# Quantised FFN, first half: groups in pairs, Gelu over two banks, rows normalised and put on the grid by GpSimd

## What is computed

```python
x = x + tanh(g_ffn[0]) * ffn(layernorm(x))
# ffn, with quantize_a16(v) = round(v * 32767 / max|v|) / (32767 / max|v|)
x_sim = quantize_a16(x)
hidden = gelu(x_sim @ W_in_sim + b_in)        # 128 -> 512
hidden_sim = quantize_a16(hidden)
out = hidden_sim @ W_out_sim + b_out          # 512 -> 128
```

## Time and profile before

| What | us |
|---|---|
| Median of 3 runs | 1489.21 (1488.17 to 1489.25) |
| Span of the profiled execution | 1487.2 |
| First half and its scale, steps at the start to the maximum (L1400 to L1427) | 616.2 to 677.1 |
| Second half (L1433 to L1444) | 678.7 to 738.5 |
| Busy over the span: TensorE, VectorE, ScalarE, GpSimd | 1444.1, 1064.9, 923.1, 640.4 |

### The profile page before, as it was taken

The page is one execution under the profiler, slowest core; times in us unless marked ns, Lnnn a source line. Parts: engine busy times, 40 slices in busy tenths (PEclk is TensorE's granted clock), DMA queues, the critical chain, the costliest instruction groups (busy, mean ns, idle before and its releaser), DMA issues. The chain is left out here.

```text
span 1487.2 us, 27490 instructions
## 1 busy us (share of the span) xinstructions
PE 1444.1 (97%) x9366; PEld 1209.9 (81%) x9384; DVE 1064.9 (72%) x2311; ACT 923.1 (62%) x1924; POOL 640.4 (43%) x755
## 2 busy tenths in 40 slices
PE   9999999999999999879999999999999999999997
PEld 8888888888888887639978888888888888778886
DVE  5677877666767678798566666666767676776887
ACT  4666666666666665496456666666666666556663
POOL 1333344343433334556023434343333333455885
PEclk9999999999999999999999999999999999999999
DMA  7655544444444442300055444444444444320011
GB/s 226 192 178 161 165 132 153 137 145 144 140 146 138 153 130 85 91 1 1 12 183 165 135 157 133 157 129 161 134 159 132 154 129 151 109 79 8 29 35 43
DMA packets 202786, 182.70 MB, mean 123 GB/s; under 512 B 12368, under 2 KB 201808, under 8 KB 202640
## 3 DMA queue, kind: packets, MB, share of 16 engines
q1 hardware_dynamic: 202080, 180.91, 38.7%
q10 hardware_dynamic: 576, 0.13, 0.1%
HBM read 95.74 MB, written 85.25 MB: 122 GB/s over the span
## 5 line engine op out<-in xcount | busy, mean ns | idle before, releaser
L1131 POOL TENSOR_TENSOR PN<-E,RC 128x512 f32<-128x512 f32 x378 | 331.2, 904 | 491.9 <-DVE RC L1089 491.9
L1038 DVE TENSOR_REDUCE MX<-pS 128x6 f32<-128x462 f32 (+1 forms) x384 | 222.6, 580 | 265.4 <-PE pS L657 265.4
L772 ACT ACTIVATE G<-pP 128x308 f32<-128x308 f32 (+1 forms) x488 | 208.9, 428 | 226.8 <-PE pP L525 226.5
L695 PE MATMUL pO<-work,PT 128*128 128x128 f32 (+1 forms) x2560 | 328.3, 276 | 4.1 <-ACT PT L856 4.1
L657 PE MATMUL pS<-G,XT 128*128 128x462 f32 (+1 forms) x768 | 321.0, 507 | 0.0
L695 PEld LDWEIGHTS pO<-work,PT 128*128 128x128 f32 (+1 forms) x2560 | 307.7, 192 | 8.4 <-issue 5.8
L847 ACT ACTIVATE E<-E 128x462 f32<-128x462 f32 (+1 forms) x384 | 209.6, 546 | 136.5 <-DVE E L1048 128.2
L523 PE MATMUL pP<-Chi,Ahi 128*128 128x308 f32 x496 | 235.2, 474 | 1.4 <-ACT G L772 1.2
L1048 DVE TENSOR_TENSOR E<-pS,MX 128x462 f32<-128x462 f32 (+1 forms) x384 | 223.6, 582 | 8.9
L856 ACT ACTIVATE PT<-pT 128x512 f32<-128x512 f32 (+1 forms) x384 | 200.2, 522 | 30.2 <-PE pT L680 28.7
L1086 DVE TENSOR_REDUCE SM<-E 128x16 f32<-128x1232 f32 (+1 forms) x144 | 184.8, 1290 | 44.7 <-ACT E L847 43.6
(11 more groups left out here) (241 smaller groups left out, 2032.7 us busy)
## 6 DMA issues: line engine op xcount, KB each, us to landing
values<-ST SPq DMA_DIRECT2D x256, 256.0 KB
work<-values SPq DMA_DIRECT2D x512, 128.0 KB
values<-ST SPq DMA_DIRECT2D x64, 208.0 KB
work<-values SPq DMA_DIRECT2D x128, 104.0 KB
C<-in_ctx SPq DMA_DIRECT2D x32, 154.0 KB
X<-in_x SPq DMA_DIRECT2D x16, 256.0 KB, 5.0
out<-s_O SPq DMA_DIRECT2D x16, 256.0 KB, 2.3
work<-in_L_xattn_Wq SPq DMA_DIRECT2D x2, 512.0 KB, 5.9
```

Of the source, the lines that this page charges most:

```text
L695: last = nc.tensor.matmul(pO[:, 0:CH], PT[0:rows, c, :], V[(t - 1) % VRING][0:rows, tile, CH * hh:CH * hh + CH], start=c == 0, stop=c == C ...
L772: return nc.scalar.activation(G[0:live, g % 2, :, head, :], bank[0:live, 0:KEYCOLS].rearrange("p (b k) -> p b k", k=KEYS), ACT.Copy)
L1038: nc.vector.tensor_reduce(MX[:, h0:h1], pS[u][:, 0:(h1 - h0) * KEYS].rearrange("p (h k) -> p h k", k=KEYS), X_AXIS, ALU.max).then_inc(max_ ...
L1131: nc.gpsimd.tensor_tensor(out, e, scale, ALU.mult).then_inc(prob_ready, 1)
```

## The change

The groups are taken in eight pairs. The sixteen up matmuls of a pair go chunk by chunk, four into two neighbouring banks `pU[c % 2]`, of which there are two sets instead of four single banks; a chunk waits for the Gelu two chunks back. One Gelu reads the 1024 columns of both banks: 32 in place of 64. Of `HI` and `LO` there are four each in place of two. TensorE turns the next pair's groups behind chunks 0 and 1, and ScalarE's `high` for them stands behind Gelus 0 and 1.

GpSimd writes each row block of 128 channels by one instruction with two values per partition (plus the negated mean, times the inverse deviation) straight into `XQ`, and then, in place over 512 columns, times the scale plus `ROUND`, which VectorE did before. The negated means are one more instruction at the start (`minus`). `XN` is gone. Groups 0 and 1 are normalised ahead of the scale.

VectorE's loop now is `low(g)`, `largest(g - 4)` for g from 2 to 15, then two more `largest`, then four reductions of 1024 columns (both groups of the last pair, a chunk each).

```diff
@@ -1211,29 +1211,31 @@
         small = sb("small", [128, 1])
         gbias = sb("gbias_f0", [128, CH])
         brow = sb("brow_f0", [128, CH])
-        amax = sb("amax", [128, GROUPS - 1 + FC])
+        PAIRS = GROUPS // 2
+        amax = sb("amax", [128, 2 * (PAIRS - 1) + FC])
+        minus = sb("minus", [128, BATCH])
 
         def half_of(i, first, n):
             return HALVES[:, i, 512 * first:512 * (first + n)]
 
-        XN = [half_of(0, i, 1).rearrange("p (b d) -> p b d", d=CH) for i in range(2)]
-        XQ = [half_of(0, 2 + i, 1).rearrange("p (b d) -> p b d", d=CH) for i in range(2)]
-        HI = [half_of(1, i, 1).bitcast(BF16)[:, 0:512] for i in range(2)]
-        LO = [half_of(1, i, 1).bitcast(BF16)[:, 512:1024] for i in range(2)]
+        XQ = [half_of(0, i, 1).rearrange("p (b d) -> p b d", d=CH) for i in range(2)]
+        parts = [half_of(0, 2, 1), half_of(0, 3, 1), half_of(1, 0, 1), half_of(1, 1, 1)]
+        HI = [h.bitcast(BF16)[:, 0:512] for h in parts]
+        LO = [h.bitcast(BF16)[:, 512:1024] for h in parts]
         raw_fc = half_of(1, 2, 1).rearrange("p (c d) -> p c d", d=CH)
         raw_proj = half_of(1, 3, 1)
         HQ = [HALVES[:, i, :].rearrange("p (c n) -> p c n", c=FC) for i in range(2)]
 
         pX = [s.enter_context(nc.psum_tensor(f"u_px{i}", [128, 512], F32)) for i in range(2)]
-        pU = [s.enter_context(nc.psum_tensor(f"u_pu{i}", [128, 512], F32)) for i in range(FC)]
+        pU = [s.enter_context(nc.psum_tensor(f"u_pu{i}", [128, 2, 512], F32)) for i in range(2)]
         pF = s.enter_context(nc.psum_tensor("pF", [128, 512], F32))
         pP = s.enter_context(nc.psum_tensor("pP", [128, 512], F32))
-        pD = pU[0:2]
+        pD = [pU[0][:, i, :] for i in range(2)]
 
...
@@ -1254,19 +1256,30 @@
         def _(pool):
             def normalise(g):
 
-                half, rows = g % 2, slice(g * GROUP, (g + 1) * GROUP)
                 if g >= 2:
-                    pool.wait_ge(xq_ready, g - 1)
-                nc.gpsimd.tensor_tensor(XN[half], p["X"][:, rows, :], p["mv"][:, rows, 0:1].to_broadcast([128, GROUP, CH]),
-                                        ALU.subtract).then_inc(centred, 1)
-                pool.wait_ge(centred, g + 1)
-                nc.gpsimd.tensor_tensor(XN[half], XN[half], p["rs"][:, rows].unsqueeze(2).to_broadcast([128, GROUP, CH]),
-                                        ALU.mult).then_inc(xn_ready, 1)
+                    pool.wait_ge(xq_turned, g - 1)
+                for b in range(GROUP):
+                    t = g * GROUP + b
+                    last = nc.gpsimd.tensor_scalar(XQ[g % 2][:, b, :], p["X"][:, t, :], minus[:, t:t + 1],
+                                                   p["rs"][:, t:t + 1], ALU.add, ALU.mult)
+                last.then_inc(xn_ready, 1)
+
+            def quantise(g):
+                pool.wait_ge(xn_ready, g + 1)
+                nc.gpsimd.tensor_scalar(XQ[g % 2], XQ[g % 2], sx[:, 0:1], ROUND, ALU.mult, ALU.add).then_inc(xq_ready, 1)
 
             nc.gpsimd.sem_clear(range(min(p["spent"]), max(p["spent"]) + 1))
+            nc.gpsimd.tensor_scalar(minus[:, :], p["mv"][:, :, 0], -1.0, 0.0, ALU.mult, ALU.add).then_inc(turned_sign, 1)
             pool.wait_ge(step_, RANGE - 1)
-            for g in range(GROUPS):
+            pool.wait_ge(turned_sign, 1)
+            normalise(0)
+            normalise(1)
+            pool.wait_ge(step_, RANGE + SCALE)
+            quantise(0)
+            quantise(1)
+            for g in range(2, GROUPS):
                 normalise(g)
+                quantise(g)
             pool.wait_ge(gbias_made, 1)
             pool.wait_ge(rounded, GROUP)
             for g in range(GROUPS):
@@ -1293,17 +1306,21 @@
             across(0)
             keep_busy(nc, p, spare, 4)
             turn(0)
-            for g in range(GROUPS):
-                if g + 1 < GROUPS:
-                    turn(g + 1)
-                pe.wait_ge(hi_out, g + 1)
-                pe.wait_ge(lo_out, g + 1)
+            turn(1)
+            for j in range(PAIRS):
+                for g in (2 * j, 2 * j + 1):
+                    pe.wait_ge(hi_out, g + 1)
+                    pe.wait_ge(lo_out, g + 1)
                 for c in range(FC):
-                    wait(pe, gelu_done, g * FC + c - FC + 1)
+                    wait(pe, gelu_done, j * FC + c - 1)
                     f = slice(128 * c, 128 * c + 128)
-                    nc.tensor.matmul(pU[c][:, :], WIN[:, f], HI[g % 2], start=True, stop=False)
-                    nc.tensor.matmul(pU[c][:, :], WIN[:, f], LO[g % 2], start=False, stop=True).then_inc(up_ready, 1)
-                if g == 1:
+                    for i in range(2):
+                        nc.tensor.matmul(pU[c % 2][:, i, :], WIN[:, f], HI[(2 * j + i) % 4], start=True, stop=False)
+                        last = nc.tensor.matmul(pU[c % 2][:, i, :], WIN[:, f], LO[(2 * j + i) % 4], start=False, stop=True)
+                    last.then_inc(up_ready, 1)
+                    if c < 2 and j + 1 < PAIRS:
+                        turn(2 * j + 2 + c)
+                if j == 0:
                     pe.wait_ge(raw_in, 32)
                     for c in range(FC):
                         n = slice(128 * c, 128 * c + 128)
@@ -1333,23 +1350,24 @@
         def _(act):
             def high(g):
                 act.wait_ge(xq_turned, g + 1)
-                if g >= 2:
-                    act.wait_ge(up_ready, (g - 1) * FC)
-                nc.scalar.activation(HI[g % 2], pX[g % 2][:, :], ACT.Copy, bias=-ROUND).then_inc(hi_out, 1)
+                if g >= 4:
+                    act.wait_ge(up_ready, (g // 2 - 1) * FC)
+                nc.scalar.activation(HI[g % 4], pX[g % 2][:, :], ACT.Copy, bias=-ROUND).then_inc(hi_out, 1)
 
             act.wait_ge(gate_in, 16)
             nc.scalar.activation(gate[:, :], gcol[:, :], ACT.Tanh).then_inc(tanh, 1)
             nc.scalar.activation(warm[:, :], gcol[:, :], ACT.Gelu)
             high(0)
+            high(1)
             act.wait_ge(up_bias_in, 16)
             act.wait_ge(scaled, 1)
-            for g in range(GROUPS):
-                if g + 1 < GROUPS:
-                    high(g + 1)
+            for j in range(PAIRS):
                 for c in range(FC):
-                    act.wait_ge(up_ready, g * FC + c + 1)
-                    nc.scalar.activation(HID[:, g, c, :], pU[c][:, :], ACT.Gelu, bias=b_in[:, c:c + 1],
+                    act.wait_ge(up_ready, j * FC + c + 1)
+                    nc.scalar.activation(HID[:, 2 * j:2 * j + 2, c, :], pU[c % 2][:, :, :], ACT.Gelu, bias=b_in[:, c:c + 1],
                                          scale=in_scale[:, c:c + 1]).then_inc(gelu_done, 1)
+                    if c < 2 and j + 1 < PAIRS:
+                        high(2 * j + 2 + c)
             act.wait_ge(raw_turned, 1)
             nc.scalar.activation(spiking["Fhi"][:, :], pF[:, :], ACT.Copy).then_inc(fhi_out, 1)
             nc.scalar.activation(spiking["WP"][:, :, :].rearrange("p c d -> p (c d)"), pP[:, :], ACT.Copy)
@@ -1380,20 +1398,15 @@
                 done(nc.vector.tensor_scalar(s[:, 1:2], s[:, 1:2], 1e-8, 1.0 / 32767.0, ALU.max, ALU.mult))
                 done(nc.vector.reciprocal(s[:, 0:1], s[:, 1:2]))
 
-            def quantise(g):
-                dve.wait_ge(xn_ready, g + 1)
-                wait(dve, xq_turned, g - 1)
-                nc.vector.tensor_scalar(XQ[g % 2], XN[g % 2], sx[:, 0:1], ROUND, ALU.mult, ALU.add).then_inc(xq_ready, 1)
-
             def low(g):
                 dve.wait_ge(hi_out, g + 1)
-                if g >= 2:
-                    dve.wait_ge(up_ready, (g - 1) * FC)
-                nc.vector.scalar_tensor_tensor(out=LO[g % 2], in0=pX[g % 2][:, :], scalar=ROUND, in1=HI[g % 2],
+                if g >= 4:
+                    dve.wait_ge(up_ready, (g // 2 - 1) * FC)
+                nc.vector.scalar_tensor_tensor(out=LO[g % 4], in0=pX[g % 2][:, :], scalar=ROUND, in1=HI[g % 4],
                                                op0=ALU.subtract, op1=ALU.subtract).then_inc(lo_out, 1)
 
             def largest(g):
-                dve.wait_ge(gelu_done, (g + 1) * FC)
+                dve.wait_ge(gelu_done, (g // 2 + 1) * FC)
                 nc.vector.tensor_reduce(amax[:, g:g + 1], HID[:, g, :, :].rearrange("p c n -> p (c n)"),
                                         X_AXIS, ALU.max, apply_absolute_value=True)
 
@@ -1404,24 +1417,22 @@
             done(nc.vector.tensor_reduce(peak[:, 0:1], up[:, :], X_AXIS, ALU.max))
             dve.wait_ge(spread, 1)
             scale_from(sx)
-            quantise(0)
             nc.vector.tensor_scalar(in_scale[:, :], inv[:, 0, :], sx[:, 1:2], None, ALU.mult).then_inc(scaled, 1)
-            quantise(1)
             low(0)
+            low(1)
             dve.wait_ge(tanh, 1)
             dve.wait_ge(bias_in, 16)
             nc.vector.tensor_scalar(gbias[:, :], brow[:, :], gate[:, 0:1], None, ALU.mult).then_inc(gbias_made, 1)
-            for g in range(GROUPS):
```

(26 more changed lines are left out.)

## The result

Median of 5 runs **1495.02 us** (1493.66 to 1496.49), the kernel before in the same comparison 1488.17 (1487.29 to 1489.25): ratio 1.0046, 95% interval 1.0035 to 1.0058. The change makes the kernel 6.9 us slower, some 0.5%; 1491.2 was forecast, with 1494.6 as the upper end of the range. The forecast was 2.0 us over 1489.21 for the kernel before, which took 1488.17 in this comparison. The profiled execution, with 1496.49 the slowest of the five, has a span of 1494.7.

A forecast was written before the change was run, and what follows sets the result against it. VectorE bound the kernel before by a hair; after, a ring of waits: Gelu 0 of pair 1 at 632.2, plus 5 x 6.36, then VectorE's queue, maximum 2.0 us later. Forecast 1491.2 us, range 1486.8 to 1494.6.

The forecast's parts named there:

- the ring: Waits through ScalarE, VectorE and TensorE, from one pair's Gelu 0 to the next: 6.36 us a pair, against 6.37 before.
- the slow side: Whole kernel slower than before by over 0.2%: chance 0.32, range up to 1494.6 us.
- the clock: TensorE's clock in the first half: 1.2 GHz for some 3.4 us at the start, costing 1.7 us of its work.
- The start: Beginning of the first half until Gelu 0 of pair 1 ends, at 632.2 us on the trace.
- the lower price: GpSimd's new instructions cost as much as its one-source casts: 0.29 us for 128 columns, 0.62 for 512; 1.8 a group.
- the upper price: GpSimd's new instructions cost as much as its two-source operations: 0.40 us for 128 columns; 2.6 a group.
- signs of being wrong: VectorE never idle at 5.6 a pair, turns waiting for GpSimd, Gelus 1.3 apart, or granted clock under 1 after 628.
- The end: After Gelu 0 of pair 6 at 664.0, VectorE works off its queue; maximum at 679.1, 2.0 us later than before.
- The rival of a bound on GpSimd: GpSimd sets the pace from 0.5 us a row beside 1.04 for the scaling; 1499 at 0.6 a row; chance 0.12.
- the clock rival: TensorE's clock falls once at the first half's end and twice in the loop, adding 3.3 us: 1494.5; chance 0.18.

The follow-up runs named there:

- run for GpSimd's prices: Kernel after with twelve more GpSimd instructions in its idle time, of 128 or 512 columns with none, one or two values per partition: 1494.4 us.

## Why the prediction was wrong, step by step

It named the mechanism, the ring, and gave the slow side too small a size and too small a chance. In the profile the half grew by 6.9 us where 2.0 was forecast. The step that failed most is the clock: the sum counted one fall at the start and put the loop at nothing, though by its own ring TensorE stands 1.6 us in each pair. The second is the price of GpSimd's values per partition, taken as nothing.

- **The ring: right, 0.16 short.** Forecast 6.36, measured 6.52 to 6.53. The part that was short is the hand-over from `low` to TensorE, 0.10 by the earlier trace rows and 0.26 here (646.24 to 646.50); why is open. Five rounds: 0.8 us. That VectorE's saving becomes its wait for `high` is in the waits above: 0.85 us a pair, 0.7 forecast. The run with the two `low` together shows the ring for cause: one edit of order, period 5.58.
- **The start: 2.1 us short, in two halves.** Gelu 0 of the second pair ends 18.05 us after the start of the half, forecast 15.96. The prediction took "the lower price" for GpSimd, 0.29 a row and 0.62 for the scaling. They come every 0.43 and 0.67 us: the row above even the upper price of 0.40, the scaling near the lower. Eight rows lie ahead of the first scaling: two groups were ready 5.9 us after the start of the half, forecast 4.5. What failed is that a value per partition was taken for free, though the same text had priced one on ScalarE at 0.09. But this profile also has 6.8 us of the lower clock at the start where 3.4 were forecast. The run for GpSimd's prices has the same code up to there and 3.4 us of it, and the same Gelu ends 17.03 us after the start of its half. So about 1.1 of the 2.1 goes with GpSimd's price, and 1.0 with the longer fall. How long the clock stays down at the start differs between profiles in which TensorE's code up to there is the same: not at all in the run with the two `low` together, 3.4 us in that for GpSimd's prices, 6.8 us here.
- **The clock: the rival, put at 0.18, came true in the loop.** The forecast counted one fall at the start. Three more came in the loop, 0.7 us each where the rival had said 0.8, 2.0 in all where it had two. Its fall at the second half, the larger part of its 3.3 us, did not come, though the filler ended 2.2 us short of the maximum (2.3 forecast). In the run with the two `low` together, where it was 4.1 us short, there was one, and it cost 2.8 us. The Trainium skill (TensorE: Matmul & The Clock Gate, A second HAM failure mode) had described such swings between matmul groups; by that rule, the trace agrees: 0.57 of full clock from 639 to 643, 1.00 from 643 to 653. A granted clock under 1 after 628 was among the prediction's own signs of being wrong.
- **The end: right.** 15.1 us from the end of Gelu 0 of pair 6 to the maximum, forecast 15.1, and the paired Gelu at 1.20 us alone and 1.10 behind another, as forecast.
- Ring 0.8, GpSimd's price 1.1, the longer fall at the start 1.0, the falls in the loop 2.0: the missing 4.9 us, of which the clock has 3.0.
- **The rival of a bound on GpSimd: wrong.** Its condition, 0.5 a row, was nearly met (0.43), but a group stays at 2.5 us under the ring's 3.26; with 0.4 us a group more nothing changed.

The lines that the start rests on are Gelu 0 of the second pair, first in the kernel after, whose half starts at 617.04, then in the run for GpSimd's prices, where it starts at 616.15:

```profile
633.88 1.21 ACT L1367 ACTIVATE HID<-u_pu,b_in,in_scale 128x1024 f32<-128x1024 f32 x1 [0.19 <-PE u_pu L1319]
```

```profile
631.97 1.21 ACT L1380 ACTIVATE HID<-u_pu,b_in,in_scale 128x1024 f32<-128x1024 f32 x1 [0.19 <-PE u_pu L1332]
```

That the measured 1495.02 lies near the clock rival's 1494.5 is in part luck: its fall at the second half, 1.7 us, did not come, and GpSimd's price and the longer fall at the start, which it did not have, made up for it.

## What to carry to other kernels

When an engine's work is made less, follow its queue once round the loop: an instruction that another engine waits for must not stand behind one that nobody waits for. Work that only has to be done by the end, as the maxima here, goes behind the hand-overs and in pieces small enough to start early, or it is all left for the end. And a pairing that halves the instructions of one engine also halves the buffer sets: look at how long the feeder then stands, and what its clock does.

## What was not expected of the hardware

- On GpSimd each operand of one value per partition cost 0.07 to 0.08 us, fixed, at 128 and at 512 columns.
- A filler in the loop took three falls of TensorE's clock away and one appeared in the second half, a part that it had not touched; whether that follows from the filler or is chance of one profile is open. Runs of one kernel differed by up to 4.7 us (1488.04 to 1492.75, ten runs of that with the longer filler), more than most effects here; why is open.
